# Set-up work split between VectorE and GpSimd, row tables moved into the set-up, and a new written-out order of steps

## The chip, the cores and the metric

The kernel runs on one core of one Trainium2 chip. The metric is the device time of one execution in microseconds; a time is the median of several runs. A profile is one further execution, recorded by the hardware; its span begins with the first instruction and ends with the last one.

## The reference

The program applies four graph layers, one after the other, to `x`, 32 graphs of 512 nodes with 128 features in float32, with one shared 512 x 512 adjacency mask `adj` (a symmetric random 0/1 matrix, denser at low indices):

- Every layer first computes `h = relu(layernorm(x))` over the features and adds its result to `x`.
- Layer 0: attention whose scores are pairs of node sums taken in an index pattern that folds the 512 x 512 grid onto itself, softmax over the rows, masked, plus `h @ self_weight`.
- Layer 1: a graph attention whose result is normalised (`h_gat`), then a graph isomorphism step `(1 + eps) * h_gat + A @ h_gat`, a two-stage MLP with layer norm and the biases `b1`, `b2`, and a residual. Its projection has the bias `bp`.
- Layer 2: graph attention with leaky relu 0.2, softmax, a bias and `elu`.
- Layer 3: `idx = cumsum(adj > 0 over the flattened matrix) - 1` picks a value `e[idx]` for every edge (`e` has 256 entries, indices beyond it take the last one), a row softmax of these values is a fixed 512 x 512 matrix A, and the result is `(A * I) h W[0] + (A * (1 - I)) h W[1] + bias`.

A of layer 3 does not depend on `x`. This document calls its construction the edge softmax.

## The kernel before, in words

The 32 graphs are worked in 16 groups of two. Six groups at most are in flight, each with its own set of tiles (slots 0 to 5). The steps of a group are in the list `STEPS` (`stat0`, `scale0`, `norm0`, ... `agg3`, `store`), with the engines that take part in each. Nothing chooses the order at run time: for every engine the string `TURNS` lists, character by character, which group takes its next step (`g` stands for the list `PREP`, the steps of the edge softmax). `HOMES` gives the PSUM bank of every tile in the order in which TensorE opens them. Each engine walks its list; semaphores make the others wait.

The program has two blocks. The first is the set-up, the second the walk through the lists. An engine enters the second block only when all engines have ended the first.

The set-up, as far as the change touches it:

- ScalarE's queue issues the loads of `WEIGHTS` and `VECTORS` (`brow`: the three bias vectors on partitions 0 and 32; `epscol`; `e_col`: the 256 values of `e`). SyncE's queue issues `adj`, the first three groups of `x` and `REST`.
- GpSimd (POOL) fills constants: `ident`, `upper`, `strict`, iotas (lines 474 to 490). It then waits for `REST` and subtracts 1 from `bias3` (line 500).
- VectorE makes the 0/1 mask `adjn` and row counts (lines 590 to 599), after the transposed mask `maskT` is there the column counts and `mask0b` (lines 607 to 617), after four tiny matmuls (`made["wvec"]`) the columns `wv`, `wcols0`, `feat1w`, `feat2w` (lines 620 to 628). Then follow, on lines 631 to 655: `e_hi`, `e_lo` (the high and low part of `e`), `bhi`, `chi`, `epsd` (1 + eps on the diagonal), `pick`, the two rows of `bias_p`, `bias_1`, `bias_2`, `diagg` (the diagonal blocks of `maskT` plus `epsd`), their high part into `gin_hi`, their low part `gin_lo`, and last `off_col`, a copy from PSUM.
- TensorE transposes the mask, sums it (`off`, `rowtot`), multiplies by `upper` for the cumulative sums `rank` (line 539, 16 matmuls of 512 columns), and last turns `off_b` into a column (line 545, `off_col`). ScalarE copies the results out: `off_b` (569), `gin_hi` (571), `rowtot_b` (573), `rank` (576).

In the second block the first step of VectorE is `erow`: from `off_col`, `cnt_row`, `rowtot_b` and `off_b` it makes the tables `row_ofT` and `row_of` (which row the m-th edge belongs to; lines 1370 to 1381). It has 14 instructions. Then VectorE takes `stat0` of three groups (line 1167) and the rest of the edge softmax: `eat` (1387 to 1394), `ecover`, `evalue` (1402, 1409, 1416), `emask` (1420 to 1425), `esoft` (1429 to 1436), `eturn` (1444). TensorE's first steps `eoffm`, `eedge`, `ecover`, `evalue` read `row_ofT` and `row_of`. ScalarE's `esoft` is line 1044, its `scale` steps are line 450. The loads of groups 3 to 5 wait for the end of `eturn`, because slots 3 to 5 use memory that the edge softmax works in.

The function `link(ins)` on VectorE and GpSimd lets an instruction count up a semaphore and makes the engine wait for it, so that the next instruction starts only when this one's result is written.

Of the kernel before, what the change touches and what calls it, by code (L numbers as in the profile page):

```python
# [30 lines left out]
P = 128  # L31
# [77 lines left out]
    ("erow", 0, "dve"),  # L109
# [10 lines left out]
    "pe": ("gggg0110101020g2120012413240303410101033114040511522553305120232123223032304143130550100001110404151"  # L120
           "4214515042454505252101321322624224226736676743472662373343234433643474684867688646786758757383757785"
           "84838848854595599599655a6a99a56a6a79799699669769657a56656a777787a78776b6ab8abb8aa67b78aab8b889798ba8"
           "bacb8cbb8c9b9dadadbc8c89dd9899ca9aaaca99ade9aecaccdeeccbcedbdcdeedb9dbdde9e9bebeebbcbecefbfffafbbcdf"
           "cfdaafffdffdfcfccceccdecddcfdfeddedffbdeeefefeffebeecffdcffbdcedfefef"),
    "act": ("g0110g2021g01244303011200341105501103015142021303221023021351033012001014114250542403105245402215314"
           "512243563222446372573644622372343473346443688668747668537537655638847748854788599755596aa9686a659798"
           "76699a76956765957997776a87ab866b6788baa77878baaa889ab9b8caac9bbd98ada8cbb898d9cab99a9adaabeeccc9cbed"
           "dcabe9cddbbce9ded9bcbeebbbcdfecfaedfacfcbdedaffdfdfcceffcdcecdeffecfdfdedffbbeedffeeefffbcdcedfcdefe"
           "fef"),
    "dve": ("g102gggg1010g0g0204131120001112234504032110330411041520352201313355422022331330045241134555000101200"  # L130
           "2414001145151412553042230451615422372242262627667633446652737673233434834764438677866484388674785788"
           "6736585783884987455799a9595956a99a98566a55799a99a6866775966a596aa77b667787767ab7ab988a6abbbc7ba8bb8a"
           "a7988bdab8cb8b889d9caabdcc8d9dc89bca9eacd9cad9aa9becca9ddce9ceeebddceeeddbabd9cae9ecbebfebdcffbffdbb"
           "fbefccffadeaffffddebcfcccefcfcdcdfdededffcddeedffeebeeffeffefcfddcbefef"),
    "pool": ("01201043120153240135234010521430510021421562374626234736847783865384547989a596a96755a679ab67687b87bc"
           "ab98da89c8adbcae9cdde9ebc9ebdabfcfafefdcdfcebfdefcdbecfdefef"),
    "sp": ("403510617228394a5b6c7d8e9fadcbef"),
}
HOMES = ("0123456701234567012347056123412341235641702356415670415067125304304356717204356072071241207431256074"
         "3612543612354072361546150723461341634613461507234615072346150723461613450726712345016273473273250164"  # L140
         "7324732432473501647235021364721364507213607452136260745264051372640513762517640325031725031371250303"
         "0643071625642565307615423073067306713540276540465270413040410310652743103146527652703140314652703146"
         "5270314652462574031640235702135647021356024756024756060612437506750567124376105246105246371052463716"
         "3710524367105721045367210721074503764076354542154207163546356435643543207165436543652407316247357325"
         "4730251673514602467351402140202673154105421607343450721625103474652103746705430546732013205467132056"
         "7420513670542136713671054240236714052367152640726341507324615073246150732461506157320461520734673461"
         "5204761532032035203524761052361470523641741760523524176035241765023764176415023415041504123765041")
# [17 lines left out]
def gnn_kernel(nc, x, adj, Wo_d, Ws_d, att0_d, Wp_d, bp_d, asrc_d, adst_d, gatg_d, gatb_d, eps_d, W1_d, b1_d,  # L165
# [12 lines left out]
    with ctx:  # L178
# [3 lines left out]
        def sem(name):  # L182
# [42 lines left out]
            "off", "off_b", "off_col", "rowtot_b", "rank")}  # L225
# [228 lines left out]
        with nc.Block() as block:  # L454
# [18 lines left out]
            def _(pool):  # L473
# [24 lines left out]

                pool.wait_ge(loaded["rest"], 16 * len(REST))
# [4 lines left out]
            def _(pe):  # L504
# [74 lines left out]
            def _(dve):  # L579
# [41 lines left out]
                link(V.tensor_copy(wv[:, 0:6], ps[2][:, 384:390]))  # L621
                V.tensor_tensor(wcols0[:, 0:1], wv[:, 0:1], wv[:, 1:2], ALU.add)
# [8 lines left out]
                V.tensor_copy(e_hi[:], e_col[:])  # L631
                V.tensor_copy(bhi[32:33], brow[32:33])
                V.tensor_copy(chi[:], wv[:, 6:7])
                link(V.tensor_scalar(small[:, 0:1], epscol[:], 1.0, None, ALU.add))
                link(V.tensor_scalar(epsd[:], ident[:], small[:, 0:1], None, ALU.mult))
                V.tensor_tensor(e_lo[:], e_col[:], e_hi[:].bitcast(F32), ALU.subtract)
                for p0 in (0, 32):
                    V.tensor_copy(pick[p0:p0 + 1, :], ones[p0:p0 + 1, :])
                for k, bias in enumerate((bias_p, bias_1, bias_2)):
                    V.tensor_copy(bias[0:1, 0:F], brow[0:1, k, :])  # L640
                    V.tensor_tensor(bias[32:33, 0:F], brow[32:33, k, :], bhi[32:33, k, :].bitcast(F32), ALU.subtract)
                V.tensor_copy(bias_p[0:1, F + 1:F + 2], wv[0:1, 6:7])
                V.tensor_tensor(bias_p[32:33, F + 1:F + 2], wv[32:33, 6:7], chi[32:33, :].bitcast(F32), ALU.subtract)
                for k in range(T):
                    a = V.tensor_tensor(diagg[:, k, :], mT[:, k, k * P:(k + 1) * P], epsd[:], ALU.add)
                link(a)
                dve.wait_ge(made["gin_hi"], 1)
                for k in range(T):
                    a = V.tensor_copy(gin_hi[:, k, k * P:(k + 1) * P], diagg[:, k, :])
                link(a)  # L650
                for k in range(T):
                    V.tensor_tensor(gin_lo[:, k, :], diagg[:, k, :], gin_hi[:, k, k * P:(k + 1) * P].bitcast(F32),
                                    ALU.subtract)
# [5 lines left out]
        with nc.Block() as block:  # L659
# [481 lines left out]
            def _(dve):  # L1141
# [227 lines left out]
                def erow(u, s):  # L1369
                    V.tensor_tensor(end_col[:], off_col[:], cnt_row[:], ALU.add)  # L1370
                    link(V.tensor_tensor(rowtot_b[:], rowtot_b[:], off_b[:], ALU.add))
                    for i in range(T):
                        V.tensor_scalar(below[:, i, :], m_row[:], end_col[:, i:i + 1], None, ALU.is_ge)
# [148 lines left out]
```

## Time and profile before

| | us |
|---|---|
| Median of 3 runs | 1014.63 |
| Lowest, highest | 1014.22, 1019.3 |
| Profiled execution, its own time | 1013.33 |
| Its span | 1011.6 |
| TensorE busy | 941.6 (93% of the span) |
| VectorE busy | 858.5 (85%) |
| ScalarE busy | 631.7 (62%) |
| GpSimd busy | 551.2 (54%) |

The profiled execution's own time is 1.7 us more than its span. In the rows below PE is TensorE's matmul, PEld its weight load, DVE is VectorE, ACT ScalarE, POOL GpSimd, SP SyncE; a "q" behind an engine's name (SPq, PEq) is its instruction queue or sequencer. L1167 is line 1167 of the kernel.

### The profile page before, as it was taken

To read this page: it belongs to the slowest core of one execution; us is meant where nothing else is said; L and a number is where in the kernel's file an instruction comes from. 1 tells how busy PE (TensorE), PEld (TensorE's weight loads), DVE (VectorE), ACT (ScalarE), POOL (GpSimd) and SP (SyncE) were. 2 spreads that over 40 slices of the span, in tenths; PEclk is the share of its full clock that TensorE was granted. 3 is DMA by queue.
4 is the path that set the end of the run, shared out by engine and by line. 5 is a ranking of instruction groups with operands and counts; after the bars stand their busy time and mean duration, and the time that the engine had idled before them with its cause. 6 is when DMAs were issued, how large, how long until landed. Compare 5 with 4: busy or idle time off the path is not lost. (4 is left out here: it accounts for less than half of the span.)

```text
span 1011.6 us, 21165 instructions
## 1 busy us (share of the span) xinstructions
PE 941.6 (93%) x7331; PEld 895.1 (88%) x7331; DVE 858.5 (85%) x2526; ACT 631.7 (62%) x1655; POOL 551.2 (54%) x1171
## 2 busy tenths in 40 slices
PE   4789999999999999999999999998999999997998
PEld 3679988988998889899989899998999898886897
DVE  6898897989879988977888888799998979779874
ACT  3346557686768653775685664877548584677741
POOL 3435274592575752755556665654636744467850
PEclk9778999999999999999999999999999999999999
DMA  5020000000020010011000101101000100000003
GB/s 136 1 63 2 1 2 1 2 1 1 2 84 2 1 43 2 1 43 44 1 1 3 41 1 43 43 2 42 2 1 2 43 1 1 22 1 1 2 1 105
DMA packets 38072, 19.99 MB, mean 20 GB/s; under 512 B 3143, under 2 KB 37453, under 8 KB 37965
## 3 DMA queue, kind: packets, MB, share of 16 engines
q1 hardware_dynamic: 36080, 18.42, 6.6%
q8 instruction: 59, 0.97, 0.4%
q10 hardware_dynamic: 1884, 0.21, 0.2%
q14 instruction: 49, 0.39, 0.1%
HBM read 10.23 MB, written 8.39 MB: 18 GB/s over the span
## 5 line engine op out<-in xcount | busy, mean ns | idle before, releaser
L685 PE MATMUL ps<-HE,PT 128*128 128x129 f32 x2048 | 238.5, 276 | 3.2 <-issue 1.9
L685 PEld LDWEIGHTS ps<-HE,PT 128*128 128x128 f32 x2048 | 233.1, 192 | 5.4 <-issue 4.9
L450 ACT ACTIVATE Y<-X,SM 128x128 f32<-128x128 f32 x512 | 204.0, 490 | 47.9 <-POOL SM L446 47.6
L1304 DVE SCALAR_TENSOR_TENSOR PT<-ps,CE,maskT 128x512 f32<-128x512 f32 x256 | 174.2, 743 | 19.3 <-PE ps L809 11.9
L431 POOL TENSOR_TENSOR SM<-ST 128x8 f32<-128x8 f32 x96 | 29.4, 306 | 267.9 <-DVE ST L1167 267.7
L442 POOL TENSOR_TENSOR SM<-SM,minus_half 128x8 f32<-128x8 f32 x96 | 162.3, 1690 | 7.6
L685 PE MATMUL ps<-W,HT 128*128 128x128 f32 (+1 forms) x768 | 126.1, 311 | 0.0
L685 PEld LDWEIGHTS ps<-W,HT 128*128 128x128 f32 x768 | 115.7, 193 | 8.9
L1167 DVE BATCH_NORM_STATS2 ST<-X 128x6 f32<-128x128 f32 x512 | 104.7, 277 | 3.3 <-DMA X<-in_x_dram 0.5
L702 PE MATMUL ps<-ident,Y 128*128 128x128 f32 x640 | 84.4, 276 | 10.6 <-ACT Y L450 10.1
L702 PEld LDWEIGHTS ps<-ident,Y 128*128 128x128 f32 x640 | 71.5, 142 | 15.8 <-ACT Y L450 14.0
L685 PE MATMUL ps<-HI,a_hi 128*128 128x256 f32 x256 | 73.2, 286 | 1.6 <-DVE LOW L1457 1.4
L955 ACT ACTIVATE HT<-ps 128x512 f32<-128x512 f32 x96 | 51.7, 596 | 35.7 <-PE ps L702 35.5
L685 PE MATMUL ps<-HI,a_lo 128*128 128x256 f32 x256 | 72.0, 281 | 0.0
L685 PE MATMUL ps<-LOW,a_hi 128*128 128x256 f32 x256 | 72.0, 281 | 0.0
L993 ACT ACTIVATE HE<-ps,HE 128x128 f32<-128x128 f32 x256 | 69.0, 382 | 0.0
L450 ACT ACTIVATE HE<-Y,SM 128x128 f32<-128x128 f32 x128 | 51.1, 496 | 27.1 <-POOL SM L446 27.0
L685 PE MATMUL ps<-gin_hi,LOW 128*128 128x512 f32 x128 | 57.8, 452 | 2.5 <-DVE X L1248 1.6
L450 ACT ACTIVATE Y<-Y,SM 128x128 f32<-128x128 f32 x128 | 51.0, 491 | 12.0 <-POOL SM L446 12.0
L1167 DVE BATCH_NORM_STATS2 ST<-Y 128x6 f32<-128x128 f32 x256 | 51.8, 275 | 6.2 <-ACT Y L1022 5.3
L1113 POOL TENSOR_TENSOR LOWB<-HE,HIB 128x1024 fp32r<-128x1024 f32 x16 | 37.7, 2358 | 30.1 <-ACT HIB L976 30.1
L685 PEld LDWEIGHTS ps<-HI,a_hi 128*128 128x128 f32 x256 | 48.5, 189 | 2.5 <-DVE LOW L1457 2.0
(258 smaller groups left out, 2315.8 us busy)
## 6 DMA issues: line engine op xcount, KB each, us to landing
X<-in_x_dram SPq DMA_DIRECT2D x32, 256.0 KB, 3.5
out_dram<-X SPq DMA_DIRECT2D x32, 256.0 KB, 2.8
adj_raw<-in_adj_dram SPq DMA_DIRECT2D x4, 256.0 KB, 4.0
W<-in_L_gnn_W_dram SPq DMA_DIRECT2D x2, 64.0 KB, 4.2
W<-in_L_gnn_W_dram SPq DMA_DIRECT2D x1, 128.0 KB, 3.9
bias<-in_L_gnn_bias_dram SPq DMA_DIRECT2D x2, 64.0 KB, 4.1
Wo<-L_gnn_others_weight_dram ACTq DMA_DIRECT2D x1, 64.0 KB, 3.1
feat1w<-in_L_gnn_Wp_dram ACTq DMA_DIRECT2D x1, 64.0 KB, 3.5
```

The lines of the kernel that those rows point to most:

```text
L431: TT(sm[:, S_DIF, :], st[:, :, 1], st[:, :, 4], ALU.subtract)
L442: link(TT(sm[:, S_RSTD, :], sm[:, S_VAR, :], minus_half[:], ALU.pow))
L450: a = nc.scalar.activation(dst[:, n, 0:F], src[:, n, 0:F], func, scale=SM[s][:, S_RSTD, n:n + 1], bias=SM[s][:, S_SHIFT, n:n + 1])
L685: return nc.tensor.matmul(o, w, m, start=start, stop=stop, skip_group_check=True)
L702: mm = T_(o[:, t * P:(t + 1) * P], Y[s][:, t * G + b, 0:F], ident[:])
L955: a = A(HT[s][:, b, :], o, ACT.Relu)
L993: a = A(HE[s][:, k, 0:F], o[:, 2 * P * b:2 * P * b + F], ACT.Identity, scale=HE[s][:, k, F:F + 1])
L1113: TT(LOB[s], VA[s], HIB[:].bitcast(F32), ALU.subtract).then_inc(sig["by_pool"][s], 1)
L1167: a = V.bn_stats(ST[s][:, n, :], src(n))
L1304: a = V.scalar_tensor_tensor(out=PT[r][:, j, :], in0=o, scalar=CE[s][:, c:c + 1], in1=maskT[:, j, :].bitcast(F32), op0=ALU.max, op1=ALU.mult)
```

## The change

There are three parts.

1. `erow` goes out of the list `PREP` and out of VectorE's first steps of the second block; its 14 instructions stand at the end of VectorE's set-up instead. For that, TensorE makes `off_col` before `rank`, not after it, and ScalarE copies `rowtot_b` before it makes `gin_hi`.
2. What VectorE did between `e_lo` and `off_col` (`bhi`, `chi`, `epsd`, `pick`, the biases, `diagg`, the diagonal blocks of `gin_hi`, `gin_lo`) is now done by GpSimd, between its iotas and the `bias3` instruction. VectorE signals `wv` with a new semaphore.
3. `TURNS` and `HOMES` are new strings. Of the lists' entries, 176 of TensorE's 469, 185 of ScalarE's 403 and 55 of GpSimd's 160 stand at another place, by seven places at most. Among the first ones: VectorE takes `stat0` of the groups 0, 2, 1 (before 1, 0, 2), ScalarE scales group 2 before the exponentials of `esoft` (before: after them), TensorE turns group 1 before group 0.

```diff
@@ POOL, set-up
+                TT, TS, copy = nc.gpsimd.tensor_tensor, nc.gpsimd.tensor_scalar, nc.gpsimd.tensor_copy
+                mT = maskT[:].bitcast(F32)
+                pool.wait_ge(loaded["vectors"], 16 * len(VECTORS))
+                link(TS(small[:, 0:1], epscol[:], 1.0, None, ALU.add))
+                link(TT(epsd[:], ident[:], wide(small[:, 0:1]), ALU.mult))
+                pool.wait_ge(made["maskT"], 2)
+                for k in range(T):
+                    a = TT(diagg[:, k, :], mT[:, k, k * P:(k + 1) * P], epsd[:], ALU.add)
+                link(a)
+                link(copy(bhi[32:33], brow[32:33]))
+                for p0 in (0, 32):
+                    link(copy(pick[p0:p0 + 1, :], ones[p0:p0 + 1, :]))
+                for k, bias in enumerate((bias_p, bias_1, bias_2)):
+                    link(copy(bias[0:1, 0:F], brow[0:1, k, :]))
+                    link(TT(bias[32:33, 0:F], brow[32:33, k, :], bhi[32:33, k, :].bitcast(F32), ALU.subtract))
+                pool.wait_ge(made["wv"], 1)
+                link(copy(chi[:], wv[:, 6:7]))
+                link(copy(bias_p[0:1, F + 1:F + 2], wv[0:1, 6:7]))
+                link(TT(bias_p[32:33, F + 1:F + 2], wv[32:33, 6:7], chi[32:33, :].bitcast(F32), ALU.subtract))
+                pool.wait_ge(made["gin_hi"], 1)
+                for k in range(T):
+                    a = copy(gin_hi[:, k, k * P:(k + 1) * P], diagg[:, k, :])
+                link(a)
+                for k in range(T):
+                    TT(gin_lo[:, k, :], diagg[:, k, :], gin_hi[:, k, k * P:(k + 1) * P].bitcast(F32), ALU.subtract)
                 pool.wait_ge(loaded["rest"], 16 * len(REST))
                 nc.gpsimd.tensor_scalar(bias3[:], bias3[:], -1.0, None, ALU.add)
@@ TensorE, set-up
+                pe.wait_ge(made["off_b"], 1)
+                for i in range(T):
+                    mm = MM(ps[2][:, N + 400 + i:N + 401 + i], off_b[:, i * P:(i + 1) * P], ident[:, 0:1], start=True, stop=True)
+                mm.then_inc(made["off_col"], 1)
                 for i in range(T):
                     for j in range(T):
                         mm = MM(ps[i // 2][:, (i % 2) * N:(i % 2 + 1) * N], maskT[:, j, i * P:(i + 1) * P],
                                 upper[:, j, :], start=(j == 0), stop=(j == T - 1))
                     if i % 2 == 1:
                         mm.then_inc(made["rank"], 1)
-                pe.wait_ge(made["off_b"], 1)
...
@@ ScalarE, set-up
                 act.wait_ge(made["maskT"], 2)
+                act.wait_ge(made["rowtot"], 1)
+                A(rowtot_b[:], ps[3][:, 0:N], ACT.Copy).then_inc(made["rowtot_b"], 1)
                 A(gin_hi[:], maskT[:].bitcast(F32), ACT.Copy).then_inc(made["gin_hi"], 1)
-                act.wait_ge(made["rowtot"], 1)
-                A(rowtot_b[:], ps[3][:, 0:N], ACT.Copy)
@@ VectorE, set-up
                 link(V.tensor_copy(wv[:, 0:6], ps[2][:, 384:390]))
+                dve.sem_inc(made["wv"], 1)
...
-                V.tensor_copy(e_hi[:], e_col[:])
-                V.tensor_copy(bhi[32:33], brow[32:33])
...
+                link(V.tensor_copy(e_hi[:], e_col[:]))
                 V.tensor_tensor(e_lo[:], e_col[:], e_hi[:].bitcast(F32), ALU.subtract)
...
+                dve.wait_ge(made["off_col"], 1)
+                link(V.tensor_copy(off_col[:], ps[2][:, N + 400:N + 400 + T]))
+                dve.wait_ge(made["off_b"], 1)
+                dve.wait_ge(made["rowtot_b"], 1)
+                V.tensor_tensor(end_col[:], off_col[:], cnt_row[:], ALU.add)
+                link(V.tensor_tensor(rowtot_b[:], rowtot_b[:], off_b[:], ALU.add))
+                for i in range(T):
+                    V.tensor_scalar(below[:, i, :], m_row[:], end_col[:, i:i + 1], None, ALU.is_ge)
+                for m in range(MB):
+                    a = V.tensor_scalar(at[:, m, :], rowtot_b[:], m_col[:, m:m + 1], None, ALU.is_le)
                 link(a)
+                for i in range(T):
+                    V.scalar_tensor_tensor(out=row_ofT[:, i, :], in0=m_row[:], scalar=off_col[:, i:i + 1],
+                                           in1=below[:, i, :], op0=ALU.is_ge, op1=ALU.subtract)
+                for m in range(MB):
+                    a = V.scalar_tensor_tensor(out=row_of[:, m, :], in0=off_b[:], scalar=m_col[:, m:m + 1],
+                                               in1=at[:, m, :].bitcast(F32), op0=ALU.is_le, op1=ALU.subtract)
+                a.then_inc(edge["rows"], 1)
@@ VectorE, second block: def erow(u, s) removed
```

## Rows read from the trace of the kernel before

**Rows 1.** The page: busy time, and TensorE's granted clock in 40 slices (tenths).
```profile
PE 941.6 (93%) x7331; PEld 895.1 (88%) x7331; DVE 858.5 (85%) x2526; ACT 631.7 (62%) x1655; POOL 551.2 (54%) x1171
...
PEclk9778999999999999999999999999999999999999
```

**Rows 2.** Stretches: length, busy us of each engine, granted clock, DMA share, GB/s.
```profile
0.00:29.36 29.36, 11.14 (x59) 9.70 (x59) 19.74 (x76) 9.63 (x25) 9.08 (x19) 0.94 0.50 117
...
400.00:600.00 200.00, 193.89 (x1512) 184.67 (x1511) 170.03 (x514) 136.67 (x358) 120.57 (x255) 0.98 0.06 17
```

**Rows 3.** Waits between 20 and 31 us: engine, line, releaser, us, times, longest.
```profile
PE ps L685 <- DVE row_of L1381: 8.3, 1, 8.3
```

**Rows 4.** The chain that ended last: a step of GpSimd between two linked instructions.
```profile
897.20 0.07 issue
```

**Rows 5.** Timeline of VectorE, 0 to 50 us: start us, us, instruction.
```profile
14.85 1.14 DVE L610 TENSOR_SCALAR mask0b<-maskT,empty 128x256 fp32r<-128x256 f32 x4
...
17.15 0.16 DVE L631 CAST e_hi<-e_col 128x2 fp32r<-128x2 f32 x1
17.32 0.35 DVE L632 CAST bhi<-brow 1x384 fp32r<-1x384 f32 x1
...
23.09 0.15 DVE L655 COPY off_col<-ps 128x4 f32<-128x4 f32 x1
23.55 0.16 DVE L1370 TENSOR_TENSOR end_col<-off_col,cnt_row 128x4 f32<-128x4 f32 x1 [0.30 <-PEq L454]
...
27.90 1.41 DVE L1381 SCALAR_TENSOR_TENSOR row_of<-off_b,m_col,at 128x512 fp32r<-128x512 f32 x2
29.23 4.73 DVE L1167 BATCH_NORM_STATS2 ST<-X 128x6 f32<-128x128 f32 x24
```

**Rows 6.** Timeline of TensorE, 0 to 48 us.
```profile
16.31 3.92 PE L539 MATMUL ps<-upper,maskT 128*128 128x512 f32 x16
20.07 0.95 PE L545 MATMUL ps<-ident,off_b 128*128 128x1 f32 x8
```

**Rows 7.** Timeline of ScalarE, 0 to 60 us.
```profile
14.72 0.68 ACT L569 ACTIVATE off_b<-ps 128x512 f32<-128x512 f32 x1
15.20 2.00 ACT L571 ACTIVATE gin_hi<-maskT 128x2048 fp32r<-128x2048 f32 x1
...
52.14 0.72 ACT L1044 ACTIVATE work<-v,rmax 128x512 f32<-128x512 f32 x1 [3.90 <-DVE rmax L1425]
```

**Rows 8.** Groups of GpSimd's instructions by shape: busy us, mean ns.
```profile
L1113 POOL TENSOR_TENSOR LOWB<-HE,HIB 128x1024 fp32r<-128x1024 f32 x16 | 37.7, 2358 | 30.1 <-ACT HIB L976 30.1
...
L434 POOL TENSOR_TENSOR SM<-SM 128x8 f32<-128x8 f32 x96 | 20.1, 210 | 7.5
...
L485 POOL TENSOR_SCALAR_AFFINE_SELECT upper<-work 128x2048 fp32r<-128x2048 f32 x1 | 1.9, 1919 | 0.0
```

**Rows 9.** Packets of ScalarE's DMA queue between 13.5 and 13.6 us, its last.
```profile
q10 hardware_dynamic: 7, 0.00, 3.9%
```

**Rows 10.** A stretch of the set-up; columns as in rows 2.
```profile
13.70:17.15 3.45, 2.68 (x16) 2.37 (x17) 2.47 (x20) 3.45 (x10) 0.00 (x0) 1.00 0.31 63
```

**Rows 11.** Timeline of VectorE between 893 and 899 us.
```profile
894.60 1.21 DVE L1318 TENSOR_TENSOR HE<-HE,gat_g 128x1024 f32<-128x1024 f32 x1
895.85 1.28 DVE L1319 TENSOR_TENSOR HE<-HE,gat_b 128x1024 f32<-128x1024 f32 x1
```

**Rows 12.** Timeline of GpSimd between 893 and 899 us.
```profile
894.76 1.11 POOL L431 TENSOR_TENSOR SM<-ST 128x8 f32<-128x8 f32 x1 [2.21 <-DVE ST L1167]
```

**Rows 13.** Timeline of GpSimd: its last instruction of the set-up, and one of the walk.
```profile
19.13 0.58 POOL L500 TENSOR_SCALAR bias<-bias 128x128 f32<-128x128 f32 x1 [9.80 <-DMA gat_b<-in_L_gnn_gat_b_dram]
...
68.61 2.96 POOL L1113 TENSOR_TENSOR LOWB<-HE,HIB 128x1024 fp32r<-128x1024 f32 x1 [7.04 <-ACT HIB L976]
```

**Rows 14.** Timeline of VectorE, 40 to 110 us.
```profile
68.31 1.22 DVE L1240 TENSOR_TENSOR LOW<-Y,HI 128x1024 fp32r<-128x1024 f32 x1
...
71.19 0.40 DVE L1216 TENSOR_TENSOR SM<-SM,CE 128x8 f32<-128x8 f32 x1
```

More of the change, by code:

```diff
@@ L108 @@
 PREP = [
-    ("erow", 0, "dve"),
     ("eoffm", 1, "pe"),
@@ L119 @@
 TURNS = {
[L120 to L128, printed above, removed]
-           "fef"),
[L130 to L134, printed above, removed]
@@ L135 @@
-    "pool": ("01201043120153240135234010521430510021421562374626234736847783865384547989a596a96755a679ab67687b87bc"
-           "ab98da89c8adbcae9cdde9ebc9ebdabfcfafefdcdfcebfdefcdbecfdefef"),
-    "sp": ("403510617228394a5b6c7d8e9fadcbef"),
-}
[L139 to L147, printed above, removed]
@@ new lines @@
+    "pe": ("gggg101000120g21120012413243003014110313440001511522553301250232122323033204413130550001001110401454"
+           "1241515425045405252101321236224224226736676743467622373343233443436447648687866486876578753778357785"
+           "88348848854559595995965a6a99a56a6a79799696699769675a65656a777787a87776b6ba8ab86aab7b78a8abb887988b9a"
+           "bcbab889bcbd9adcadbdcc8d989899aca9aaca99d9eaacecacdeecbccedbdcdeebd9dbdde9e9bebbbeceebcefbffffbabcdf"
+           "cfadafffdffdfcfcccecdcedcdcffdeddedffbdeeefeffefbeefefcdcffbdcedfefef"),
@@ L224, in gnn_kernel @@
             "pool", "adjn", "maskT", "turn", "WT_ps", "WT", "rowtot", "bprep", "wvec", "gin_hi", "counts",
-            "off", "off_b", "off_col", "rowtot_b", "rank")}
+            "off", "off_b", "off_col", "rowtot_b", "rank", "wv")}
         edge = {n: sem("edge_" + n) for n in ("rows", "at", "masked", "exp", "soft", "hi", "done")}
@@ L542, in _ @@
                         mm.then_inc(made["rank"], 1)
-                pe.wait_ge(made["off_b"], 1)
-                for i in range(T):
-                    mm = MM(ps[2][:, N + 400 + i:N + 401 + i], off_b[:, i * P:(i + 1) * P], ident[:, 0:1], start=True, stop=True)
-                mm.then_inc(made["off_col"], 1)
             @block.scalar
@@ L630, in _ @@
                 dve.wait_ge(loaded["vectors"], 16 * len(VECTORS))
-                V.tensor_copy(e_hi[:], e_col[:])
-                V.tensor_copy(bhi[32:33], brow[32:33])
-                V.tensor_copy(chi[:], wv[:, 6:7])
-                link(V.tensor_scalar(small[:, 0:1], epscol[:], 1.0, None, ALU.add))
-                link(V.tensor_scalar(epsd[:], ident[:], small[:, 0:1], None, ALU.mult))
-                V.tensor_tensor(e_lo[:], e_col[:], e_hi[:].bitcast(F32), ALU.subtract)
-                for p0 in (0, 32):
-                    V.tensor_copy(pick[p0:p0 + 1, :], ones[p0:p0 + 1, :])
@@ L639, in _ @@
[L639 to L645, printed above, removed]
@@ L646, in _ @@
-                link(a)
[L647 to L653, printed above, removed]
-                dve.wait_ge(made["off_col"], 1)
-                V.tensor_copy(off_col[:], ps[2][:, N + 400:N + 400 + T])
+                link(V.tensor_copy(e_hi[:], e_col[:]))
@@ L1367, in elu2 @@
                                                 op1=ALU.add))
[L1369 to L1373, printed above, removed]
-                    for m in range(MB):
-                        a = V.tensor_scalar(at[:, m, :], rowtot_b[:], m_col[:, m:m + 1], None, ALU.is_le)
-                    link(a)
-                    for i in range(T):
-                        V.scalar_tensor_tensor(out=row_ofT[:, i, :], in0=m_row[:], scalar=off_col[:, i:i + 1],
-                                               in1=below[:, i, :], op0=ALU.is_ge, op1=ALU.subtract)
-                    for m in range(MB):
-                        a = V.scalar_tensor_tensor(out=row_of[:, m, :], in0=off_b[:], scalar=m_col[:, m:m + 1],
-                                                   in1=at[:, m, :].bitcast(F32), op0=ALU.is_le, op1=ALU.subtract)
-                    a.then_inc(edge["rows"], 1)
                 def eat(u, s):
@@ L1474, in _ @@
                 run = {
-                    "erow": erow, "eat": eat, "ecover": ecover, "evalue": evalue, "emask": emask,
+                    "eat": eat, "ecover": ecover, "evalue": evalue, "emask": emask,
                     "esoft": esoft, "eturn": eturn,
```

21 lines of the change are left out of this document (added).

## The prediction

> **What bounds the kernel now.** I read the page first, then the stretches, then the waits and the timelines of the first 60 us. The page shows TensorE busy for 941.6 us, 93% of the span, and no other engine above 85% [rows 1]. The stretches say where the missing 70 us lie: of the first 29.36 us TensorE works 11.14, so 18.2 us are idle there, while between 400 and 600 us it works 193.9 of 200 [rows 2]. The reader is to see two regimes: a start in which TensorE waits for others, and a long middle in which it is the bound. Whatever starts the middle earlier should move the end by as much, as nothing in it hangs on a fixed time: the loads of the later groups wait for the edge softmax, which moves along.
>
> The start is a chain. TensorE's last idle stretch, 8.3 us, is a wait for `row_of`, the last table of `erow` [rows 3]. VectorE runs without a gap into it: `e_hi` at 17.15, the moved set-up work from 17.32, `off_col` at 23.09, then 0.30 us for the change of blocks, `erow` from 23.55 to 29.31, and `stat0` [rows 5]. TensorE had ended its own set-up at 21.02 [rows 6], ScalarE a little later. So VectorE sets this stretch alone, while GpSimd does one instruction of 0.58 us after an idle time of 9.8 us [rows 13].
>
> **Part 1, VectorE.** Between 17.32 and 23.09 its instructions go (26 of them) except `e_lo`, and `off_col` moves up. `off_b` is copied by 15.40 [rows 7], and TensorE is free for it after its tiny matmuls at 16.3; the 8 `off_col` matmuls take 0.95 us [rows 6] and end at 17.3. VectorE ends `e_lo` at 17.5, so the new wait costs nothing or 0.1. `off_col` ends at 17.75, `erow` takes 5.76 (23.55 to 29.31) [rows 5], so VectorE's set-up ends at 23.5, if nobody disturbs it. `rowtot_b` needs no wait: it goes ahead of `gin_hi`, from 15.2 or 15.7 for 0.7 us. The moved `gin_hi` ends at 17.9 instead of 17.2 [rows 7], and only GpSimd waits for it. `rank` starts and ends 0.95 us later on TensorE, at about 21.2, and ScalarE's copy of it at 22.2; both are before 23.5 and cost nothing. If the rest were free, the second block would start at 23.5 + 0.3 with `stat0` in place of `erow`: 23.8 against 29.23, 5.4 us earlier. That is the most that the part can bring.
>
> **Part 2, GpSimd.** It has 27 instructions now, 26 new ones and `bias3`. The trace has none of these shapes on GpSimd, but rows on both sides. Two inputs: 2.358 us for 1024 elements and 0.210 for 8 [rows 8], so 0.0021 us an element and 0.46 for 128. One input: 1.919 for 2048 elements [rows 8], from the same foot 0.31 for 128 and 0.53 for 384. The sum: 12 with two inputs of 128 (`epsd`, 4 `diagg`, 3 biases, 4 `gin_lo`) 5.6; 10 with one input of 128 (2 `pick`, 3 biases, 4 `gin_hi`, `bias3`) 3.1; `bhi` 0.5; four tiny ones 0.8; together 10.0. Sixteen links add 0.07 each [rows 4], 1.1, and the instructions without one overlap a little, -0.4: 10.7 us. It starts when `VECTORS` have landed: the queue's last packets are at 13.5 to 13.6 [rows 9], so at 13.7. Its waits for `maskT`, `wv` and `gin_hi` (14.3, 16.8, 17.9) fall before it gets there. Undisturbed it ends at 24.4, 0.9 us after VectorE, and is the new end of the set-up: 24.7 with the change of blocks.
>
> It will not be undisturbed. When VectorE runs two instructions with two inputs in SBUF, GpSimd's 8-element instruction that should take 0.21 takes 1.11: it ends with VectorE's, at 895.87 against 895.81 [rows 11, 12]. The other way round, a VectorE instruction of 8 elements lasts 0.40 where small ones last 0.16 [rows 5]: it ends at 71.59, as GpSimd's long one does at 71.57 [rows 13, 14]. That long one had itself lost 0.6 (2.96 against 2.36 on average [rows 8]) behind VectorE's of 68.31 to 69.53. `bias3` in the set-up took 0.58 where I work out 0.31, so it lost 0.27 beside VectorE's instructions of 0.2 to 0.3.
>
> The Trainium skill states the rule for this (SBUF — State Buffer, "Who interferes with whom"): VectorE in a two-port mode, or with two SBUF inputs against a reading GpSimd, and GpSimd exclude each other for whole instructions. The 1.11 us agrees. The rule speaks against this change, since nearly all of `erow` is of these kinds; taken to the letter it is the third rival below, and without any exclusion the sum would stay at 24.7.
>
> The bounds: nothing lost, 24.4; every busy microsecond of VectorE's lost to GpSimd. That is 2.5 between 13.7 and 17.15 [rows 10], 0.5 for the rest up to `off_col`, and 5.7 for `erow`, so 8.7, and the end is at 33.1. My value: about 14 of the 27 instructions meet a dense VectorE, at 0.2 us each (the 0.27 of `bias3` is the nearest row; early on VectorE is busy only 2.5 of 3.45 us), so 2.8. GpSimd ends at 27.2; VectorE, held in its turn, at some 24.5, hidden below that. The second block starts at 27.5 instead of 29.23: **1.7 us gained**.
>
> **Part 3, the order.** TensorE's idle time outside the first 29.36 us is 52 us [rows 1, 2], and a new order can only work on that and on the granted clock, which is at 0.7 to 0.9 in the first two slices and 1.0 nearly everywhere after the fourth [rows 1]. One gain can be seen: ScalarE stands idle for 3.9 us before the exponentials of `esoft` [rows 7], and `scale0` of group 2 now fills that hole. Its eight activations leave the stretch in which TensorE waits for the first groups. But TensorE is busy there at the lower clock, so most of it is hidden. For all other moves (at most seven places, mostly one) I can't derive a sum; the bounds I set at -4 and +4 us, 8% of the idle time either way. I take 1.5 us gained, since the visible move is in that direction.
>
> **Sum.** 1.7 + 1.5 = 3.2 us off the profiled execution's 1013.3, 1010.1. The median of the runs is 1.3 us above that execution; on it the forecast is 1011.4.
>
> **The rivals.** (a) GpSimd works nearly undisturbed, for instance as its instructions on one partition and VectorE's short ones pass between each other. Then the block starts at 24.7, 4.5 us gained, with the order 6.0: 1008.6. For it: `bias3` lost only 0.27 us in a stretch as dense as `erow`. Against it: the 0.9 us lost in [rows 11, 12]. (b) The order alone brings 4 where I take 1.5: 1008.9. Nothing in the profile excludes it. (c) The other side: GpSimd becomes the bound of the set-up and loses all that VectorE works, so that the block starts at 33.4, 4.2 us later than now. With a neutral order this is 1018.8. It turns from gain to loss where GpSimd ends after 28.9. For it: the exclusion seen in the rows, and 27 instructions which each can arrive behind one of `erow`'s 0.3 to 0.7 us. Against it: exclusion should cover the moving of data only, not the fixed part of each instruction, and VectorE leaves gaps. (d) The new order loses: a wait such as that of TensorE for `cmax0` or `norm1` grows, 4 us lost with 1.7 gained: 1016.9. (e) `erow` moves but the edge softmax's later steps are held by something else: the first of them, `eoffm`, waits only for `row_of`, so I give this no chance of its own.
>
> **How the numbers follow.** Forecast with 1 to 5 us gained: 0.5. (a) 0.18, (b) 0.1, (c) 0.12, (d) 0.1. The forecast's own range is 1009.6 to 1013.6. With (a), (b) and most of (c) and (d) the range for 8 in 10 is 1006.5 to 1017.5. Faster by over 0.5% means below 1009.6 (0.5%, 5.1 us, is about what a measurement can tell from no change): all but a little of (a) and (b), 0.26. Slower by over 0.5% means above 1019.7: the ends of (c) and (d), 0.06. The rest is 0.68.
>
> **What would show it.** In the changed kernel's timeline `end_col` begins near 17.8 and VectorE's last set-up instruction ends at 23.5 to 25; `gin_lo` and `bias3` on GpSimd are the last of the set-up, near 27; the first `stat0` starts at about 27.5; TensorE's wait for `row_of` becomes one for the change of blocks of some 6 us. GpSimd's copies of 128 elements show about 0.3 undisturbed and 0.5 or more beside `erow`. From 60 us on, each step of the first groups should come 2 to 3 us earlier. The forecast is wrong if VectorE's instructions in `erow` stretch so much that it ends after GpSimd, if the start of the block is outside 25 to 29, or if the start moves as said and TensorE's idle time after it does not stay within 4 us of 52.

## The result, and the profile after

| | before | after |
|---|---|---|
| Median, us | 1014.91 (1014.22 to 1019.3, 4 runs) | 1035.24 (1027.58 to 1036.67, 4 runs) |
| Profiled execution: span, us | 1011.6 | 1034.8 |
| TensorE busy, us | 941.6 | 964.6 |
| Mean granted clock of TensorE | 0.980 | 0.957 |

The ratio is 1.0169 (95% interval 1.0140 to 1.0198): slower, where 0.3% faster was forecast. In a second measurement, on another chip, it was 1.0105 (1.0068 to 1.0143), from single times of 1022 to 1035 us. The changed kernel scatters more than the one before: over its ten executions the time goes with TensorE's mean granted clock, from 1022.1 us at 0.974 to 1036.7 at 0.957. The kernel before has two clusters in all its measurements, 1013 to 1017 us at a clock of 0.975 to 0.980 and 1018 to 1022 at 0.969 to 0.974, so a ratio below can differ by up to 0.3% from the quotient of the two medians.

The page of after shows TensorE's busy time 23 us longer with the same 7331 matmuls, and the lower clock in more of the 40 slices; in [rows 1] nearly all of it is in the first four.

```profile
PE 964.6 (93%) x7331; PEld 915.4 (88%) x7331; DVE 856.5 (83%) x2500; ACT 633.0 (61%) x1655; POOL 557.8 (54%) x1197
...
PEclk9758899999999998999998999999999989999999
```

The granted clock accounts for the 23 us. Means of 0.980 and 0.957 are some 41 and 89 us at the lower of its two levels, 1.2 instead of 2.4 GHz, and half of the 48 us more is 24 (an estimate from these rows). The idle time of TensorE is 70.2 us against 70.0, so by its sum the new order costs nothing. That sum hides something: split by stretches, in the section on the prediction, it is 4.8 us longer in one place and shorter in others.

The set-up went much as forecast. The timelines of GpSimd and VectorE in after (start us, us, instruction) answer to [rows 5, 9, 13]:

```profile
14.76 0.25 POOL L501 TENSOR_SCALAR small<-epscol 128x1 f32<-128x1 f32 x1 [5.40 <-DMA e_col<-in_L_gnn_e_dram]
15.10 0.40 POOL L502 TENSOR_TENSOR epsd<-ident,small 128x128 f32<-128x128 f32 x1
...
22.71 1.82 POOL L519 CAST gin_hi<-diagg 128x128 fp32r<-128x128 f32 x4
24.61 2.64 POOL L522 TENSOR_TENSOR gin_lo<-diagg,gin_hi 128x128 fp32r<-128x128 f32 x4
27.22 0.55 POOL L524 TENSOR_SCALAR bias<-bias 128x128 f32<-128x128 f32 x1
```
```profile
15.56 2.02 DVE L634 TENSOR_SCALAR mask0b<-maskT,empty 128x256 fp32r<-128x256 f32 x4
...
19.76 0.24 DVE L662 TENSOR_TENSOR end_col<-off_col,cnt_row 128x4 f32<-128x4 f32 x1
...
24.73 1.79 DVE L673 SCALAR_TENSOR_TENSOR row_of<-off_b,m_col,at 128x512 fp32r<-128x512 f32 x2
28.11 4.74 DVE L1187 BATCH_NORM_STATS2 ST<-X 128x6 f32<-128x128 f32 x24 [1.58 <-PEq L453]
```

GpSimd is the new end of the set-up, at 27.77. Beside it VectorE is slower than in before: `mask0b` takes 2.02 instead of 1.14 us, `row_of` 1.79 instead of 1.41 [rows 5]. The second block's `stat0` starts at 28.11 instead of 29.23.

The large difference is behind that. VectorE's `top1` and `top2` steps occur once per group, so their starts serve as milestones. Times of the profiled executions, us (the kernels of the lower rows are told below):

| | top1 gr. 0 | top1 gr. 6 | top2 gr. 6 | top2 gr. 7 | top2 gr. 15 | span |
|---|---|---|---|---|---|---|
| before | 102.96 | 387.35 | 531.23 | 566.55 | 942.38 | 1011.6 |
| after | 110.62 | 395.35 | 543.46 | 586.15 | 965.19 | 1034.8 |
| difference | 7.7 | 8.0 | 12.2 | 19.6 | 22.8 | 23.2 |
| changed kernel, again | 104.04 | 388.99 | 534.51 | 577.06 | 954.22 | 1023.5 |
| GpSimd's ten turns put back | 106.76 | 391.59 | 537.10 | 572.66 | 948.54 | 1018.2 |
| old order, GpSimd's ten turns new | 103.30 | 388.10 | 533.29 | 580.44 | 960.78 | 1030.0 |

Two places stand out: 7.7 us are lost before 111 us, and 7.4 us in the one stretch from `top2` of group 6 to `top2` of group 7. Here is that stretch in after, first VectorE, then GpSimd, then TensorE:

```profile
543.00 0.43 DVE L1304 TENSOR_REDUCE MX<-ps 128x2 f32<-128x256 f32 x1 [0.51 <-PE ps L820]
543.46 2.29 DVE L1308 TENSOR_TENSOR CF<-DS,MX 128x8 f32<-128x8 f32 x1
545.67 4.50 DVE L1310 TENSOR_SCALAR CF<-DS,MX 128x4 f32<-128x4 f32 x2
550.08 1.22 DVE L1260 TENSOR_TENSOR LOW<-Y,HI 128x1024 fp32r<-128x1024 f32 x1
```
```profile
541.39 1.89 POOL L1140 TENSOR_TENSOR HT<-SR,norow 128x1024 f32<-128x1024 f32 x1 [4.84 <-ACT SR L1019]
543.36 2.36 POOL L1142 TENSOR_TENSOR HT<-HT,bias 128x1024 f32<-128x1024 f32 x1
545.68 2.34 POOL L1147 TENSOR_TENSOR X<-X,bias 128x1024 f32<-128x1024 f32 x1
547.98 2.16 POOL L1133 TENSOR_TENSOR LOWB<-HE,HIB 128x1024 fp32r<-128x1024 f32 x1
```
```profile
551.41 1.08 PE L829 MATMUL ps<-ident,CE 128*128 128x128 f32 x4 [4.88 <-ACT HT L971]
```

`top2` ends with three tiny instructions of 4 or 8 elements. Each of them ends with one of GpSimd's long ones (545.75 with 545.72, the last at 550.17 with 550.14): 6.7 us for what takes 0.44 in before. ScalarE's exponentials wait for them, TensorE waits 4.88 us, and its clock is at the lower level from 549.8 to 556.6 us. GpSimd's order is the cause by its look: `mean2` of group 6 (L1140, L1142) now stands ahead of `shift3` (L1147) and `low0` (L1133), so four long instructions run in one row, beginning just when `top2` of the same group is due. The old order has the same four in a row, but `shift3` leads and has to wait for ScalarE, so the row begins 1.2 us after VectorE has finished its step:

```profile
531.23 0.17 DVE L1288 TENSOR_TENSOR CF<-DS,MX 128x8 f32<-128x8 f32 x1
531.32 0.35 DVE L1290 TENSOR_SCALAR CF<-DS,MX 128x4 f32<-128x4 f32 x2
```
```profile
532.83 2.35 POOL L1127 TENSOR_TENSOR X<-X,bias 128x1024 f32<-128x1024 f32 x1 [7.43 <-ACT Y L450]
```

The stretch from `top2` of group 6 to that of group 7, before and after (columns as in [rows 2]), shows that most of the 7.4 us is waiting: TensorE's idle time in it goes from 1.0 to 5.8 us, its busy time from 34.3 to 36.8.

```profile
531.23:566.55 35.32, 34.30 (x277) 32.78 (x276) 29.19 (x85) 17.33 (x47) 19.67 (x36) 1.00 0.11 31
```
```profile
543.46:586.15 42.69, 36.84 (x280) 35.58 (x279) 36.53 (x86) 18.80 (x49) 16.76 (x35) 0.92 0.09 26
```

### The profile page after: what moved, and what is told of

Read it like the earlier page. It is cut to its first block and busy times, and to the rows that moved or that the text cites. A ratio compares the mean times of both kernels' runs of the same rounds, so it can differ in the third digit from the quotient of the medians.

```text
span 1034.8 us, 21171 instructions
## 1 busy us (share of the span) xinstructions
PE 964.6 (93%) x7331; PEld 915.4 (88%) x7331; DVE 856.5 (83%) x2500; ACT 633.0 (61%) x1655; POOL 557.8 (54%) x1197
## 5 line engine op out<-in xcount | busy, mean ns | idle before, releaser
L705 PE MATMUL ps<-HE,PT 128*128 128x129 f32 x2048 | 241.1, 277 | 4.2 <-issue 2.8
L449 ACT ACTIVATE Y<-X,SM 128x128 f32<-128x128 f32 x512 | 203.7, 489 | 35.6 <-POOL SM L445 35.6
L1324 DVE SCALAR_TENSOR_TENSOR PT<-ps,CE,maskT 128x512 f32<-128x512 f32 x256 | 174.3, 743 | 19.1 <-PE ps L829 10.8
L430 POOL TENSOR_TENSOR SM<-ST 128x8 f32<-128x8 f32 x96 | 26.4, 275 | 264.1 <-DVE ST L1187 263.9
L705 PE MATMUL ps<-W,HT 128*128 128x128 f32 (+1 forms) x768 | 128.2, 315 | 0.9 <-ACT HT L975 0.8
L722 PEld LDWEIGHTS ps<-ident,Y 128*128 128x128 f32 x640 | 72.2, 143 | 15.2 <-ACT Y L449 12.7
L1133 POOL TENSOR_TENSOR LOWB<-HE,HIB 128x1024 fp32r<-128x1024 f32 x16 | 37.4, 2335 | 34.5 <-ACT HIB L996 34.4
L1187 DVE BATCH_NORM_STATS2 ST<-Y 128x6 f32<-128x128 f32 x256 | 51.8, 275 | 4.8 <-ACT Y L1042 3.2
L705 PE MATMUL ps<-gin_hi,HI 128*128 128x512 f32 x128 | 50.9, 398 | 0.0
```

The source lines that it names most:

```text
L430: TT(sm[:, S_DIF, :], st[:, :, 1], st[:, :, 4], ALU.subtract)
L449: a = nc.scalar.activation(dst[:, n, 0:F], src[:, n, 0:F], func, scale=SM[s][:, S_RSTD, n:n + 1], bias=SM[s][:, S_SHIFT, n:n + 1])
L705: return nc.tensor.matmul(o, w, m, start=start, stop=stop, skip_group_check=True)
L722: mm = T_(o[:, t * P:(t + 1) * P], Y[s][:, t * G + b, 0:F], ident[:])
L1133: TT(LOB[s], VA[s], HIB[:].bitcast(F32), ALU.subtract).then_inc(sig["by_pool"][s], 1)
L1187: a = V.bn_stats(ST[s][:, n, :], src(n))
```

## The experiments

Ratios are to the kernel before on the same chip, with 95% intervals.

**First: which part?** Order and set-up are taken apart; each edit is one of the parts of the change, alone.

```diff
order_only:  before.TURNS, HOMES  ->  after's ("g" kept in front of VectorE's, erow in PREP)
setup_only:  after.TURNS, HOMES   ->  before's (without that "g")
erow_only:   before, erow/off_col/rowtot_b in the set-up; biases and diagonal stay on VectorE
pool_only:   before, biases and diagonal on GpSimd; erow stays in the walk
(the last two with after's sequence on TensorE and ScalarE: off_col ahead of rank, rowtot_b ahead of gin_hi)
```

> The kernel before with the changed kernel's TURNS and HOMES alone; erow stays VectorE's first step of the walk and the set-up is that of before. Theory O (the new order thins out TensorE's work between 50 and 115 us, so the chip grants the lower clock for some 90 us instead of 40): 1030 to 1037 us, mean clock near 0.957, TensorE busy near 965 us. Theory S (the set-up moves the start, and what follows meets the clock at another moment): 1013 to 1016, clock 0.98. Theory B (both are needed): 1013 to 1020.

> The changed kernel's set-up with the TURNS and HOMES of before (without the g of erow). Theory O: 1013 to 1015 us, clock 0.98, the second block starting 1.1 us earlier than before. Theory S: 1027 to 1037, clock 0.957 to 0.967. Theory B: 1013 to 1020.

> Only erow, off_col and rowtot_b moved into the set-up; VectorE keeps the biases and the diagonal, order of before. VectorE does the same instructions in the same sequence, so the second block starts at 29.2 us with stat0. All theories but S: within 1 us of before. Theory S in its wide form (any shift of a few tenths changes the clock's steps): some us either way.

> GpSimd makes biases and the diagonal's parts, erow stays the first step of the walk, order of before. GpSimd now meets a nearly idle VectorE from 19.7 us on, so it should end at 25.0 to 26.5 instead of 27.8, and erow's 5.7 us come after it: stat0 at 31 to 32.5 instead of 29.2, 2 to 3 us slower than before, 1016 to 1018, if the clock stays.

| | median, us | ratio | stat0 starts, us |
|---|---|---|---|
| order_only | 1029.29 | 1.0113 (1.0076 to 1.0150) | 29.27 |
| setup_only | 1014.89 | 0.9968 (0.9945 to 0.9992) | 27.61 |
| erow_only | 1016.80 | 1.0007 (0.9989 to 1.0024) | 29.73 |
| pool_only | 1018.53 | 1.0009 (0.9986 to 1.0032) | 30.61 |

The order is what makes the kernel slower; TensorE is busy for 957.1 us in it, at a clock of 0.963. The set-up alone is a little faster, by 0.3% as a ratio but only 0.4 us between the medians; neither half of it alone shows a gain. The starts of `stat0` say why: `erow` has to be somewhere, and only when GpSimd takes work off VectorE does it become free. The loss of 2 to 3 us forecast for `pool_only` is neither shown nor excluded, as its interval reaches up to 0.32% and its median is 3.2 us above.

**Second: where in the order?** At a cut near 115 us both orders have done the same steps and every PSUM bank has the same last tile, so pieces can be joined. The set-up is after's in all that follow.

```diff
old115_new:  order = old[:cut] + new[cut:]   (cut: TensorE 57, ScalarE 35, VectorE 43, GpSimd 18 steps)
new115_old:  order = new[:cut] + old[cut:]
old75_new:   the same with TensorE 22, ScalarE 14, VectorE 20, GpSimd 12 steps of the old order
fill_waits:  new order; in cmax0 and coefb0 the tile opened ahead of the wait, and there for group 0
+                        for n in range(26):   # 17 in coefb0
+                            nc.tensor.matmul(o[:, 256:512], maskT[:, 0, 0:P], maskT[:, 1, 0:256], ...)
```

> The changed kernel with the old order up to about 115 us (TensorE's first 57 steps, ScalarE's 35, VectorE's 43, GpSimd's 18) and the new one behind it; the same steps stand on both sides of the cut and all eight PSUM banks have the same last tile there. Theory E (the clock is lost in the new order's first 115 us, and what comes later is noise or follows from it): 1015 to 1020 us. Theory L (the later drops of the clock, between 250 and 970 us, are the new order's own): 1025 to 1030.

> The changed kernel with the new order up to about 115 us and the old one behind it. Theory E: 1027 to 1035 us. Theory L: 1020 to 1025, since 20 us more at the lower clock before 115 us cost 10 us. If both halves add up (10 from the start, 13 from the rest), this run is 1023 to 1026 and the other 1025 to 1029.

> Old order only for TensorE's first 22 steps (up to agg0 of group 1, feat0 of group 2), the new one from there. In the new order feat0 of group 1 comes late, so that turns, 4-column and 128-column matmuls fill 62 to 75 us at the lower clock, before agg0's 256-column ones. If that stretch is the seed, the lower clock from 73 to 90 us in the trace's count goes back to 7 us and the run is 5 to 9 us below the changed kernel: 1026 to 1030. If the order further on matters alone: 1033 to 1037.

> The changed kernel, and TensorE does 26 and 17 extra matmuls of 256 columns into unread columns of the tiles of cmax0 and coefb0 of group 0, ahead of its waits of 3.3 and 2.0 us. Theory W (idle waits make the clock fall there): the drops near 51 and 62 us vanish or shorten, and 8 to 12 us come back, 1023 to 1028. Theory N (the narrow matmuls between are what keeps it low): the drops stay and the time is 1035 to 1038.

| | median, us | ratio |
|---|---|---|
| old115_new | 1026.46 | 1.0091 (1.0057 to 1.0124) |
| new115_old | 1019.47 | 1.0032 (1.0012 to 1.0053) |
| old75_new | 1027.90 | 1.0122 (1.0075 to 1.0169) |
| fill_waits | 1025.33 | 1.0094 (1.0062 to 1.0126) |

My theory E, that the start is all, falls: by the medians the part behind 115 us costs more (11 us) than the start (4 us), and together they make 15 us, between the two measurements of the changed kernel (20 and 11). Both are counted from the kernel before, so each has the gain of the set-up already in it. `old75_new` came out as forecast (1026 to 1030), but it cannot be told from the changed kernel's second measurement, so it decides nothing. `fill_waits` has the clock of before (0.981) and is still 9 us slower in the profile, so the clock alone does not explain the loss either. It and `old115_new` hold the same TensorE wait of 4.9 us as after; this is its row in `old115_new`, waits of TensorE between 500 and 560 us:

```profile
PE ps L808 <- ACT HT L950: 4.9, 1, 4.9
```

**Third: the place at 543 us.** Ten of GpSimd's 160 turns are put back; nothing else.

```diff
 GpSimd's turns 81 to 90, after:  6:stat2 5:stat3 7:mlps1 6:mean2 5:shift3 10:low0 9:gats1 7:stat2 ...
+put back to:                     6:stat2 7:mlps1 5:stat3 5:shift3 10:low0 6:mean2 7:stat2 9:gats1 ...
```

> The changed kernel with only ten of GpSimd's 160 turns (the 81st to the 90th) in the old order, so that mean2 of group 6, shift3 of group 5 and low0 of group 10 no longer stand in one row of four long instructions. Theory X (VectorE's three tiny instructions of a top step are held behind them one by one, 6.3 us in all, and TensorE's 4.9 us wait and a drop of the clock follow): the 4.9 us wait goes and the time falls by 5 to 9 us against the changed kernel. Rival: the wait moves to the next place where GpSimd is late, and nothing is gained.

Seven of the ten stand at another place. The median is 1019.40 us, ratio 1.0044 (1.0023 to 1.0066). VectorE and GpSimd in its profile, at the same step:

```profile
537.10 0.17 DVE L1287 TENSOR_TENSOR CF<-DS,MX 128x8 f32<-128x8 f32 x1
537.19 0.36 DVE L1289 TENSOR_SCALAR CF<-DS,MX 128x4 f32<-128x4 f32 x2
```
```profile
539.09 2.36 POOL L1126 TENSOR_TENSOR X<-X,bias 128x1024 f32<-128x1024 f32 x1 [6.01 <-ACT Y L428]
```

The three tiny instructions take 0.45 us again, GpSimd's row begins 1.5 us behind them, the 4.9 us wait is gone, and the way to `top2` of group 7 takes 35.6 us as in before (35.3) instead of 42.7. Then the other direction, with the base once more on the same chip, and the two repairs joined:

```diff
old_new_seg_b:      old order everywhere, GpSimd's turns 81 to 90 in the new one
pool_seg_fill_b:    ten turns put back + the extra matmuls of fill_waits
pool_seg_old115_b:  ten turns put back + the old order up to 115 us
```

> The changed kernel once more, so that the others of this call stand beside it on one chip. 1028 to 1037 us. If it is under 1024, the chip and not the edit made the difference between it and the run with ten of GpSimd's turns put back.

> The set-up of the changed kernel with the order of before, and only GpSimd's turns 81 to 90 in the new order: the reverse of the run before. If the row of four long GpSimd instructions is enough to hold VectorE's top2 of group 6, this is 4 to 8 us slower than the set-up alone (1014.9): 1019 to 1023, with an instruction of over 1 us in line CF<-DS,MX near 531 us. If VectorE's own place matters as much (in the old order it reaches top2 at another moment against mean2), it stays within 2 us of 1015.

> The changed kernel with GpSimd's ten turns put back and the 26 and 17 extra matmuls ahead of the first waits. If collision and start are the two causes and add up, 1014 to 1018 us, no slower than before by more than 0.3%. If the extra matmuls only shifted where the clock fell, 1018 to 1022.

> The changed kernel with GpSimd's ten turns put back and the old order up to 115 us. If the two are all that the new order costs, it is the set-up alone, 1014 to 1016. What is left above 1015 is what the other moves behind 115 us cost; the steps between top1 of group 4 and top2 of group 2 suggest 1 to 4 us.

| | median, us | ratio |
|---|---|---|
| changed_b | 1026.31 | 1.0105 (1.0068 to 1.0143) |
| old_new_seg_b | 1030.64 | 1.0132 (1.0111 to 1.0154) |
| pool_seg_fill_b | 1017.46 | 1.0016 (0.9994 to 1.0039) |
| pool_seg_old115_b | 1016.68 | 1.0004 (0.9987 to 1.0022) |

`changed_b` lies under the expected 1028 to 1037, but over the 1024 below which the chip and not the edit would have made the difference. In the old order the ten turns alone cost 15 us, where I expected 4 to 8, and more than they do in the new one. VectorE, GpSimd and TensorE there:

```profile
530.48 2.44 DVE L1322 SCALAR_TENSOR_TENSOR LOW<-HE,HI 128x1024 fp32r<-128x1024 f32 x1
...
533.29 1.86 DVE L1287 TENSOR_TENSOR CF<-DS,MX 128x8 f32<-128x8 f32 x1
535.07 4.50 DVE L1289 TENSOR_SCALAR CF<-DS,MX 128x4 f32<-128x4 f32 x2
```
```profile
529.34 2.50 POOL L1119 TENSOR_TENSOR HT<-SR,norow 128x1024 f32<-128x1024 f32 x1 [4.99 <-ACT SR L998]
531.91 3.21 POOL L1121 TENSOR_TENSOR HT<-HT,bias 128x1024 f32<-128x1024 f32 x1
```
```profile
540.82 1.09 PE L808 MATMUL ps<-ident,CE 128*128 128x128 f32 x4 [5.46 <-ACT HT L950]
```

Here VectorE's step before it is held too (2.44 instead of 1.22 us), and in turn stretches GpSimd's to 3.21. From `top2` of group 6 to that of group 7 it takes 47.2 us, 11.8 more than in before, and 3.8 more come before `top1` of group 10. The stretch (columns as in [rows 2]) has 10.2 us of idle time where before has 1.0:

```profile
533.29:580.44 47.15, 36.92 (x268) 35.80 (x269) 34.47 (x85) 15.75 (x43) 15.21 (x33) 0.89 0.08 23
```

So these turns of GpSimd are enough. The loss need not lie in TensorE's busy time either: over the whole execution that is 948.2 us here, 6.6 more than in before, and the idle time 81.8, 11.8 more.

The last two rows of the table say that this and the start are most of the loss, not all of it. With both repaired the kernel stands with the one before, but it has the new set-up too, so the yardstick is `setup_only`: 0.9968 against 1.0004, some 3 us, with intervals that just meet, and its forecast was 1014 to 1016. In its profile `pool_seg_old115_b` is 5.0 us behind `setup_only` at `top2` of group 7 (571.0 against 566.1) and 2.9 at the end. That the extra matmuls repair the start is suggested, not shown: `pool_seg` without them has 1.0044, with an interval that overlaps.

**Fourth: what the start loses, and whether there is more to win.** TensorE at the same steps of the new order, in the profile of after and then in the second profile of the same kernel (`changed_b`); behind each timeline stands a stretch of it (columns as in [rows 2]):

```profile
62.74 3.67 PE L909 MATMUL ps<-ident,v 128*128 128x128 f32 x16
66.20 3.42 PE L705 MATMUL ps<-wcols,HT 128*128 128x4 f32 x16
69.48 3.76 PE L705 MATMUL ps<-Wo,HT 128*128 128x128 f32 x16
```
```profile
66.00:74.00 8.00, 8.00 (x40) 8.00 (x39) 7.12 (x20) 3.11 (x6) 2.83 (x5) 0.50 0.57 158
```
```profile
60.28 1.96 PE L909 MATMUL ps<-ident,v 128*128 128x128 f32 x16
62.08 1.95 PE L705 MATMUL ps<-wcols,HT 128*128 128x4 f32 x16
63.89 2.03 PE L705 MATMUL ps<-Wo,HT 128*128 128x128 f32 x16
```
```profile
62.00:66.00 4.00, 4.00 (x38) 4.00 (x37) 3.73 (x7) 1.30 (x6) 0.72 (x4) 1.00 0.05 12
```

The same matmuls, without a gap in either: at 1.2 GHz (0.50) in one execution, at 2.4 GHz (1.00) in the other. In after the clock fell at 61.7, right behind the 1.98 us wait that ends at 61.31, and came back only at 78.7, when the first 16 matmuls of `agg0` of group 0 had run (256 columns each, from 74.9); in between TensorE was busy throughout. In before it is lower from 66.6 to 73.4, and it fell there during a wait of 2.7 us. So at `top1` of group 0 the changed kernel is between 1 and 8 us late (104.0 to 110.6 against 103.0), by where the clock falls in that execution.

Three kernels try to keep the clock up, all with the set-up of after and the order of before:

```diff
 setup_fill, at the end of TensorE's set-up:
+                for n in range(56):
+                    MM(ps[3][:, N:N + 256], maskT[:, 0, 0:P], maskT[:, 1, 0:256], start=True, stop=True)
 setup_fill2: and 22 such matmuls ahead of the wait of cmax0 of group 2
 setup_fill3: and 8 such matmuls each in coef0 of the groups 0 and 1
```

> The set-up of the changed kernel with the order of before, and 56 extra matmuls of 256 columns at the end of TensorE's set-up, into a PSUM bank that nothing reads any more. They fill 6.0 of the 6.3 us in which TensorE waits for the second block. If the clock falls because TensorE idles there, the drop of 10 us behind it goes or shrinks, and eoffm and eedge run at the full clock: 2 to 4 us faster than the set-up alone. If the narrow matmuls that follow let it fall anyway: no difference, or 0.5 us slower.

> As the one before, and 22 extra matmuls ahead of the 2.7 us wait of cmax0 of group 2, near 66 us. If that wait causes the drop of 6.8 us behind it: a further 2 to 3 us faster. If not: the same within 0.5 us.

> As the one before, and 8 extra matmuls of 256 columns spread over the 16 pairs of 4-column matmuls of coef0, for groups 0 and 1: 1.7 us of work on TensorE's path. If the 4-column matmuls are what the chip takes for idleness at 49.5 to 56.4 us, up to 3.4 us come back, net 1.5 to 2 faster than the one before. If not: 1 to 1.7 us slower.

| | median, us | ratio |
|---|---|---|
| setup_fill | 1013.76 | 0.9980 (0.9964 to 0.9997) |
| setup_fill2 | 1015.13 | 0.9985 (0.9968 to 1.0002) |
| setup_fill3 | 1016.91 | 1.0008 (0.9991 to 1.0026) |

The first does what it should: `eoffm` takes 1.96 instead of 3.57 us, at the full clock from its start.

```profile
28.20 1.96 PE L707 MATMUL ps<-off_col,row_ofT 128*128 128x1 f32 x16 [0.45 <-PEq L453]
```

But the 2 to 4 us that I expected beside `setup_only` (0.9968) are not to be seen: the ratio is no lower, and the medians, taken on two chips, are 1.1 us apart. Part of the gain goes to the extra matmuls: they end at 27.75, 0.8 us after GpSimd's set-up. The second adds no gain, the third loses about the work that it adds. Where the faster stretch is given back was not isolated. The best of all kernels that ran are `setup_only` and `setup_fill`, 0.3% and 0.2% under the kernel before.

## Why the prediction was wrong

**The set-up (parts 1 and 2): right, with its sizes, one of them partly by luck.** `end_col` came at 19.76, not 17.8. Of the 2.0 us, 0.5 are the mask, which came later in this execution; for most of the rest VectorE was held by GpSimd from 15.2 us on, which I had counted only against GpSimd. It was hidden, as said, since GpSimd ended last. GpSimd started at 14.76 instead of 13.7, as `e_col` landed later, and took 13.0 us where I had 10.7 + 2.8. In `pool_only`, where VectorE stands idle from 18.8 us on, it took 10.8, so the 10.7 was right within 0.1 and the disturbance was 2.2. That my 2.8 came near is that luck: its nearest row was `bias3`, said to have lost 0.27 us beside VectorE, but in `pool_only` it takes 0.55 us with VectorE idle, so the 0.58 in before was about its own price:

```profile
24.03 0.55 POOL L525 TENSOR_SCALAR bias<-bias 128x128 f32<-128x128 f32 x1
```

The block started at 28.1 (27.3 in the second profile), in the stated 25 to 29, and the gain was 1.1 to 1.9 us against 1.7. Rivals (a) and (c) are out. With the old order the start brought 0.32%, 0.08 to 0.55%.

**The order (part 3): this step failed.** I bounded it at 4 us either way as "8% of the idle time", since the moves are small. The prediction names the granted clock beside the idle time as what an order can work on, and then puts it at nothing. (It also speaks of two slices at 0.7 to 0.9, where [rows 1] has four.) The size was wrong and so was what it was taken from. A rearrangement within ten turns of GpSimd's list costs 7 us in the new order (by the milestones of its two profiles) and 15 us in the old one. And in sum the idle time stayed at 70 us: the loss shows in the busy time, 964.6 against 941.6, because waits of 2 to 5 us are followed by stretches at the lower clock, in which every matmul takes up to twice as long. I had the means: [rows 11 to 14] show the exclusion of VectorE and GpSimd, and I applied it to the set-up only, not to the 64 long GpSimd instructions of the walk, whose turns the change moves. The prediction's own test ("TensorE's idle time after it does not stay within 4 us of 52") would have passed (it is 54.0, against 51.8 in before), while the forecast was 24 us off.

The one gain that I could see came as a move, not as time. `scale0` of group 2 ran at 47.6 us instead of 55.0, and ScalarE's idle time before the exponentials went from 3.9 to 1.7, but TensorE was 7.7 us late at `top1` of group 0 all the same.

**The rivals.** (b) is out with the order's loss. (d), the new order loses, was the right one, with the wrong price: 4 us and a chance of 0.1. Its mechanism is there: TensorE waits 3.3 us for `cmax0` of group 0, where before waits 0.3 for the first two groups' and 2.7 for group 2's, and the 2.0 us wait for `coefb0` of group 0 is new. But over the stretch up to `top1` of group 0 its idle time grows by 0.7 us only; the rest is the clock. A loss of over 0.5% had a chance of 0.06.

**The sum.** How much longer each stretch is in the profiled execution of after, us, and how much of it is TensorE's busy and idle time:

| up to | longer | busy | idle |
|---|---|---|---|
| `stat0` of the walk | -1.1 | +0.9 | -2.0 |
| `top1` of group 0 | +8.8 | +8.1 | +0.7 |
| `top1` of group 6 | +0.3 | +0.5 | -0.2 |
| `top2` of group 6 | +4.2 | +3.2 | +1.1 |
| `top2` of group 7, the collision | +7.4 | +2.5 | +4.8 |
| `top2` of group 15 | +3.2 | +7.4 | -4.2 |
| the end | +0.4 | +0.4 | 0.0 |
| all | 23.2 | 23.0 | 0.2 |

The second row has 20 us more at the lower clock, which by itself would be 10. The 4.2 us hold a smaller hit of the same kind, at `top1` of group 8 (453.7 us: 1.71 instead of 0.17 us); that one is read from the trace and was not tried alone. What makes the last 3.2 us is open; a stretch at the lower clock from 839.9 to 850.1 us lies in it, which `old115_new`, `changed_b` and `pool_seg_fill_b` have too, `fill_waits` and `pool_seg` not, so it does not come with the collision.

## What to carry to other kernels

When a change touches an order, walk the list of the long GpSimd instructions and look at which VectorE steps of a few elements fall beside them. Four in a row stood in both orders here; what differed was whether the first of them was ready before VectorE's step or after it. What counts is not how busy the engines are but whether the tiny step is one that ScalarE and TensorE wait for. Split a change into its parts before explaining it: the set-up, to which nearly the whole working of the prediction went, made 1 to 2 us, and the part that could not be worked out made 14 when it was tried alone. And where TensorE is the bound, compare its busy time for the same instructions as well as its idle time, and both by stretches: the sum of the idle time was the same here, and a wait of 5 us was in it.

## What the runs showed of the hardware

- Three VectorE instructions of 4 or 8 elements took 6.7 us beside GpSimd's row of 1024-element instructions, and 0.44 us without. Each is held anew, by one GpSimd instruction: they end at 545.75, 548.05 and 550.17 us, GpSimd's at 545.72, 548.02 and 550.14. The Trainium skill (SBUF — State Buffer, "Who interferes with whom") states that one of the two blocks for the other's whole instruction; the 2.29 and 4.50 us agree.
- The hold goes both ways in one place: VectorE's 2.44 instead of 1.22 us, and GpSimd's 3.21 instead of 2.36.
- The clock stayed at the lower level for 17 us in which TensorE was busy 17.7 of 18 us, over transposes and matmuls of 4 and 128 columns and, from 74.9 us on, of 256 (0.53 between 61 and 79 us). The same steps of the same kernel ran at 1.00 in another execution.
- With extra matmuls before two waits the clock is higher as a whole: 0.970 to 0.981 over the seven executions of `fill_waits`, 0.957 to 0.974 over the ten of the changed kernel. `setup_fill` shows that a clock won need not be time won.
